# A graph network in four layers: the node pass between second and third layer taken out, edge states kept densely, the third layer in two stages

## The chip, the cores and the metric

The kernel runs on one core of a Trainium2 chip. The metric is the device time of one execution in microseconds (us), the median of several runs. The engines of the core are PE (matrix multiplication and transposes), DVE (vector), ACT (scalar, with tables for its functions), POOL (general) and SP (issues DMAs only). They run their own instruction streams and wait for one another by semaphores.

## The reference

There are 100,000 nodes with 64 numbers each and 50,000 edges, sorted by destination. Four layers follow one another, each of them as x = x + layer(relu(layernorm(x))):

```
x = x + gat(h, edges)                       # layer 0: softmax over the edges of a destination, tanh
x = x + gelu(batchnorm(gatv2(h)) + h)       # layer 1: softmax by destination, 16 edge attributes
x = x + rpe(h):                             # layer 2: softmax by SOURCE, 18 edge attributes
    qkv = h @ qkv_w + qkv_b
    compat = (q[s]*scale + ea @ q_rpe) . (k[t] + ea @ k_rpe)
    attn = segment_softmax(compat, s);  out = segment_sum((v[t] + ea @ v_rpe) * attn, s)
x = x + rgcn(h):                            # layer 3: twice a sum of messages by destination and a GRU,
    msg = (h[src] @ weight[type]) * norm;  state = gru(segment_sum(msg, dst), state)
    batchnorm over all nodes
```

The batch norms of layers 1 and 3 need a mean and a variance over all nodes, so what follows them can only start when every edge of the layer is done. A node without edges in a layer still gets the layer's value for an empty sum.

## The kernel before, in words

Edges are taken in chunks of CE = 512: 128 partitions with TPC = 4 edges each, 98 chunks (NCH). Nodes are taken in 32 chunks of 3200: 128 partitions with 25 rows each. Each stage below is one block of the program; the next one starts when it has ended. In a stage every engine has a loop over the chunks, written with `slots(eng, total, lags, body)`: in turn n the body is called with chunk n, n-1, n-2 and so on, so that the steps of neighbouring chunks overlap. The order of instructions on an engine is the order of the lines in its body; nothing reorders it.

The stages are: preparation (lists of edges by destination and by source, sorted on the chip); `conv_gat` (layer 0); `conv_gatv2` (layer 1); `nodes_second`, a pass over all nodes; `conv_rpe` (layer 2); `conv_first` and `conv_rgcn` (layer 3, in two rounds, called l3a and l3b in the traces); `nodes_last`, a pass over all nodes.

Rows of a node table are fetched by POOL with indirect DMAs (`Rows.gather`, L864), four to a chunk and list, and written back by indirect DMAs (`Scatter.scatter`, L897), four to a chunk. Both have four buffers. All other transfers are issued by SP, one after another in the order of its body; the last pass stores from ACT.

`conv_gatv2` gathers x1 by source, takes the destination's state from the last stage, computes attention, and scatters the result o1 to the nodes; it sums o1 and its squares for the batch norm. On its way it joins the 18 edge attributes with the destination numbers in one table (L1378, L1379) and fills two other tables with rest values. `nodes_second` loads x1 and o1 of every node, makes the layer norm of x1, the batch norm of o1, their sum, the Gelu and x2, and stores x2 twice (table x2, and the left half of table xh). Beside it POOL gathers the attributes of the edges in the order by source (L1559). `conv_rpe` gathers x2 of source and of the other end (two lists, in the order by source), norms them, multiplies with qkv_w (L1755) and the edge attributes with the position weights (L1756), makes the softmax by source with scans on DVE (L739, L813), adds x2, makes the layer norm of the result as well and scatters both as 128 numbers to xh. `conv_first` gathers 64 normed numbers from xh and does the first round of layer 3; `conv_rgcn` the second, and scatters its states to g2. `nodes_last` loads xh and g2 and stores the output.

In `Norm`, `square` (L675) runs on ACT, `rsqrt` (L685, L686) on ACT as Ln and Exp; `load_ln_exp` (L203) loads the table of these two functions.

## Time and profile before

| what | value |
|---|---|
| runs | 7380.1, 7376.67, 7300.94 us; median 7376.67 us |
| profiled execution | 7345.78 us, its span 7344.1 us |
| busy: PE, DVE, ACT, POOL | 3808.4 (52%), 5219.6 (71%), 2420.3 (33%), 5506.7 us (75%) |
| DMA | 647.68 MB, 88 GB/s mean, 846543 packets, 656112 of them under 512 B |
| chain that ended last | only the end of the last pass: DMA 2%, POOL 1%, DVE 1% |

The busy shares are means over stages which have different limits. Since a stage starts when the one before it has ended, the span is the sum of the stages, and each stage can be read by itself from its own stretch of time. The span minus the sum of the windows is below 0.2 us; the profiled execution's time is 1.7 us longer than its span.

### The profile page before, as it was taken

How to read it: one execution, taken by the hardware profiler on the slowest of the kernel's cores; microseconds unless marked ns; L12 is line 12 of the kernel's file. 1: busy time of each engine (PE TensorE's matmuls, PEld its weight loads, DVE VectorE, ACT ScalarE, POOL GpSimd, SP SyncE). 2: the span in 40 equal slices, each digit the busy share in tenths (PEclk: the TensorE clock that was granted, in tenths of full speed). 3: DMA queues.
4: the chain of work that ended last, by engine and by line, in shares of the span. 5: the costliest groups of instructions: out<-in, count | busy, mean ns of one | idle time of the engine just before them, and what ended most of it. 6: DMA issues, size and time to landing. Idle time of an engine off the chain costs nothing. (4 is left out here: it accounts for less than half of the span.)

```text
span 7344.1 us, 70844 instructions
## 1 busy us (share of the span) xinstructions
PE 3808.4 (52%) x11974; PEld 2014.6 (27%) x11974; DVE 5219.6 (71%) x9194; ACT 2420.3 (33%) x5053; POOL 5506.7 (75%) x5757
## 2 busy tenths in 40 slices
PE   0103444553677777000166666666668877777700
PEld 0001111111233333000044444444434434444400
DVE  5885777776799998898066666666667767777644
ACT  1113444443444444333033333333323323333300
POOL 4777888887677777788778888888667767777745
PEclk9999555555677777555555555555589988888855
DMA  3442222222454544676111111111123322222258
GB/s 98 133 126 66 73 73 73 73 74 69 117 122 122 122 122 126 185 217 174 14 44 41 43 41 43 43 41 43 38 69 90 89 63 48 48 48 48 47 175 247
DMA packets 846543, 647.68 MB, mean 88 GB/s; under 512 B 656112, under 2 KB 684269, under 8 KB 846271
## 3 DMA queue, kind: packets, MB, share of 16 engines
q1 hardware_dynamic: 691399, 463.53, 22.5%
q0 software_dynamic: 150560, 157.85, 10.3%
q10 hardware_dynamic: 4512, 25.60, 1.1%
q14 instruction: 59, 0.48, 0.0%
q8 instruction: 13, 0.21, 0.0%
HBM read 385.69 MB, written 274.56 MB: 90 GB/s over the span
## 5 line engine op out<-in xcount | busy, mean ns | idle before, releaser
L864 POOL DMA_INDIRECT l_rows<-x,l_num x1176 | 1241.0, 1055 | 333.3 <-issue 324.1
L1559 POOL DMA_INDIRECT er_edge_rows<-eat,all_perm x392 | 539.3, 1376 | 144.9 <-issue 131.4
L897 POOL DMA_INDIRECT xh<-l_out,l_snum x392 | 432.3, 1103 | 162.9 <-issue 104.8
L864 POOL DMA_INDIRECT l_rows<-in_x,l_num x392 | 440.5, 1124 | 106.3 <-issue 90.6
L1102 POOL DMA_INDIRECT pre_src_rows<-in_x,all_idx_src x392 | 396.8, 1012 | 163.9 <-issue 130.3
L897 POOL DMA_INDIRECT x<-l_out,l_snum x392 | 410.2, 1047 | 106.6 <-issue 89.4
L864 POOL DMA_INDIRECT l3a_rows<-xh,l3a_num x392 | 389.3, 993 | 133.7 <-issue 98.1
L897 POOL DMA_INDIRECT o<-l_out,l_snum x392 | 393.8, 1005 | 122.8 <-issue 104.7
L897 POOL DMA_INDIRECT g<-l3b_out,l3b_snum x392 | 393.5, 1004 | 107.0 <-issue 89.1
L864 POOL DMA_INDIRECT l3b_rows<-g_rows,l3b_num x392 | 386.7, 987 | 106.2 <-issue 91.7
L1729 PE MATMUL l_p_ea<-all_ident,l_ea 128*32 128x128 f32 x392 | 99.1, 406 | 704.6 <-ACT l_ea L1644 697.9
L1288 PE MATMUL l_p_hT<-all_ident,l_h 128*128 128x128 f32 x392 | 109.4, 435 | 528.2 <-DVE l_h L671 528.2
L675 ACT ACTIVATE l_n_sq<-l_n_cen 128x512 f32<-128x512 f32 (+1 forms) x392 | 223.9, 571 | 353.8 <-DVE l_n_cen L662 284.0
L1747 PE MATMUL l_p_score<-l_vT,all_w_head 68*128 68x512 f32 x196 | 200.3, 1126 | 265.2 <-DVEq L746 265.2
L821 PE MATMUL l_p_sums<-all_ident,l_sums 128*128 128x128 f32 x1176 | 300.0, 405 | 47.9 <-DVE l_sums L783 32.3
L1756 PE MATMUL l_p_qkv<-all_w_rpe,l_eaT 19*128 19x128 f32 x784 | 310.5, 497 | 0.0
L1755 PE MATMUL l_p_qkv<-all_w_qkv,l_hT 128*128 128x128 f32 x784 | 296.1, 481 | 0.9 <-ACT l_hT L1662 0.9
L2135 PE MATMUL l3b_p_gate<-all_w_gate,l3b_acc 128*128 128x256 f32 x784 | 284.5, 526 | 20.3 <-DVEq L2086 18.6
L2182 POOL TENSOR_TENSOR dl_xin<-dl_xin,all_shift 128x1600 f32<-128x1600 f32 x32 | 150.8, 4721 | 175.9 <-DMA dl_gin<-g 175.8
L2127 PE MATMUL l3b_p<-all_ident,l3b_hm 128*128 128x128 f32 x392 | 138.9, 370 | 257.3 <-DVEq L2079 257.3
L821 PEld LDWEIGHTS l_p_sums<-all_ident,l_sums 128*128 128x128 f32 x1176 | 203.5, 205 | 226.7 <-DVE l_sums L783 191.9
L1741 PE MATMUL l_p_hT<-all_ident,l_h 128*128 128x128 f32 x392 | 100.0, 405 | 312.2 <-DVEq L1708 312.2
(384 smaller groups left out, 12444.3 us busy)
## 6 DMA issues: line engine op xcount, KB each, us to landing
l_far<-far_d SPq DMA_DIRECT2D x196, 256.0 KB, 3.5
x<-ts_row SPq DMA_DIRECT2D x31, 812.5 KB, 4.4
d_xrow<-x SPq DMA_DIRECT2D x31, 812.5 KB, 4.5
l_far<-far_s SPq DMA_DIRECT2D x98, 256.0 KB, 3.4
o<-l_fill_o SPq DMA_DIRECT2D x97, 256.0 KB
g<-l_fill SPq DMA_DIRECT2D x97, 256.0 KB
xh<-l_fill_h SPq DMA_DIRECT2D x97, 256.0 KB
ts_xin<-in_x SPq DMA_DIRECT2D x31, 800.0 KB, 5.8
```

Source lines behind the costliest of these rows:

```text
L675: act.activation(self.sq[:], self.cen[:], ACT.Square).then_inc(self.squared, 1)
L821: ins = pe.transpose(self.p_sums[:, j * P:(j + 1) * P], self.sums[k.u][:, j * P:(j + 1) * P], c.ident[:])
L864: pool.indirect_dma_start(self.buf[k.q][:, j, at:at + w], None, table, bass.IndirectOffsetOnAxis(ap=self.num[k.q][:, m, j:j + 1], axis=0)) ...
L897: pool.indirect_dma_start(self.table, bass.IndirectOffsetOnAxis(ap=self.num[k.q][:, j:j + 1], axis=0), self.out[k.q][:, j, 0:self.cols], N ...
L1102: pool.indirect_dma_start(c.src_rows[:, t, :], None, x, bass.IndirectOffsetOnAxis(ap=c.idx_src[:, t:t + 1], axis=0)).then_inc(c.src_gather ...
L1559: pool.indirect_dma_start(c.edge_rows[:, t, :], None, eat, bass.IndirectOffsetOnAxis(ap=c.perm[:, t:t + 1], axis=0)).then_inc(c.edges_gath ...
L1747: pe.matmul(p_score[:], c.w_head[:], vT[k1.u][:], start=True, stop=True).then_inc(m["scored"], 1)
L1755: pe.matmul(p_qkv[:, at], hT[:, at], c.w_qkv[:], start=True, stop=False)
L1756: ins = pe.matmul(p_qkv[:, at], eaT[0:19, at], c.w_rpe[:], start=False, stop=True)
L2127: pe.transpose(p_01[:, cols], hm[:, j, 0:P], c.ident[:])
L2135: ins = pe.matmul(p_gates[:, j, :], acc[k1.u][:, j * P:(j + 1) * P], w_gate[:], start=True, stop=True)
L2182: pool.tensor_tensor(xin[k.u][:], xin[k.u][:], over_rows(c.shift3[0:NP, :], NR), ALU.add).then_inc(pool_done, 1)
```

## The change

The change takes `nodes_second` out and makes what it computed where it is needed:

- `conv_gatv2` no longer scatters o1. It stores three dense tables in the order of the edges by destination: xs (the gathered x1 of source and destination with its position), hs (their normed states) and eo1 (the result of the destination after each edge). It does not fill tables and does not join attributes. h has two buffers.
- A new stage `conv_edges` (l2 in traces) goes over the edges by destination. It gathers eo1 for the source of each edge, loads the other five inputs densely, makes batch norm, Gelu, x2 and its layer norm for both ends of each edge, carries the destination's row along with a scan, multiplies qkv and position weights, and stores x2 of both ends (x2e) and, for each edge, value and compatibility (vc_rows, 68 numbers).
- A new stage `conv_source` (l2s) gathers vc_rows in the order by source, makes the softmax and scatters the message sum to m2. Beside it, a class `Default` makes x2 for all nodes as if they had no edge in layer 1 (8 rows in each partition per turn) and stores it with the rest state of layer 3 to xg.
- `conv_first` gathers m2, adds the dense x2, and makes the layer norm. `conv_second` (the former second round) scatters x2 and state together, 128 numbers, to xg. `nodes_last` reads xg and m2 and has three operations in place of two on DVE.

The diff, cut to its core (`hold` is a wait together with an instruction that does nothing):

```diff
 def conv_gatv2 ... SP:
+                        if not k.round:
+                            hold(sp, rows.rows_free, k.n - 4)
+                            hold(sp, rows.saved[k.q], 16 * k.r)
...
+                    if old:
+                        hold(sp, rows.rows_free, old.n)
+                        sp.dma_start(edge_rows(xs, old), rows.buf[old.q][:]).then_inc(rows.saved[old.q], 16)
+                        hold(sp, m["h_ready"], old.n)
+                        sp.dma_start(edge_rows(hs, old), h[old.u][:]).then_inc(h_saved[old.u], 16)
+                    if older:
+                        hold(sp, kept.out_ready, older.n)
+                        sp.dma_start(edge_rows(eo1, older), kept.out[older.q][:, :, 0:D]).then_inc(o_saved[older.q], 16)
 POOL:
-                gather_scatter(pool, c, rows, sct, 7)
+                gather_scatter(pool, c, rows, None, 0)
 ACT:
-                act.wait_ge(attr_loaded, 32)
-                act.activation(attr_out[:, :, 0:ATTR], attr_in[:], ACT.Copy).then_inc(attr_joined, 1)
...
-def nodes_second(nc, c, x1, o1, x2, xh, eat):
...
-def conv_rpe(nc, c, dram, x2, xh):
...
+def conv_edges(nc, c, dram, eo1, xs, hs, edge_attr, x2e, vc_rows):
+        vc = [s.sb(f"vc{u}", [P, TPC, VC]) for u in range(2)]
...
 conv_edges, SP:
+                def body(k, _1, old, _3, _4, older):
+                    if k:
+                        ea.load(sp, c, k)
+                        if not k.round:
+                            hold(sp, rows.rows_free, k.n - 4)
+                        sp.dma_start(rows.buf[k.q][:, :, D:P], edge_rows(eo1, k)).then_inc(own_loaded[k.q], 16)
...
+                        sp.dma_start(x1[k.u][:], edge_rows(xs, k)).then_inc(x1_loaded[k.u], 16)
+                    if old:
+                        hold(sp, m["x2_ready"], old.n)
+                        sp.dma_start(edge_rows(x2e, old), x2[old.u][:]).then_inc(x2_saved[old.u], 16)
+                    if older:
+                        hold(sp, m["vc_ready"], older.n)
+                        sp.dma_start(edge_rows(vc_rows, older), vc[older.u][:]).then_inc(vc_saved[older.u], 16)
+                slots(sp, c.NCH, 5, body)
...
 conv_edges, ACT:
+                def body(k0, k1, k2):
+                    if k2:
+                        act.wait_ge(m["h_turned"], k2.n)
+                        act.activation(hT[k2.u][0:D, :], p_hT[0:D, :], ACT.Copy).then_inc(m["src_out"], 1)
+                    if k1:
+                        norm.square(act, k1.n)
+                        ea.copy_out(act, k1.n)
+                        norm.rsqrt(act, step, c, k1.n)
+                    if k2:
+                        act.wait_ge(m["qkv_done"], k2.n)
+                        if not k2.first:
+                            act.wait_ge(m["vc_ready"], k2.n - 2)
+                            act.wait_ge(vc_saved[k2.u], 16 * k2.t)
+                        v = p_qkv[:].rearrange("p (j f) -> p j f", j=TPC)
+                        act.activation(qk[k2.u][:], v[:, :, 0:D], ACT.Copy)
+                        act.activation(vc[k2.u][:, :, 0:D], v[:, :, D:P], ACT.Copy).then_inc(m["qkv_out"], 1)
+                    if k0:
+                        act.wait_ge(m["z_ready"], k0.n)
+                        act.activation(z[:], z[:], ACT.Gelu).then_inc(m["gelu_done"], 1)
+                        load_ln_exp(nc, act)
...
 conv_edges, PE:
+                def body(k1, k2):
+                    if k2:
...
+                            pe.matmul(p_qkv[:, at], hT[k2.u][:, at], c.w_qkv[:], start=True, stop=False)
+                            ins = pe.matmul(p_qkv[:, at], ea.T[0:ATTR + 1, at], c.w_rpe[:], start=False, stop=True)
+                        ins.then_inc(m["qkv_done"], 1)
+                    if k1:
+                        ea.turn(pe, c, k1)
+                        hold(pe, m["h_ready"], k1.n)
...
 class EdgeAttr, load(sp, c, k), the first transfer of SP's turn:
-            sp.wait_ge(self.turned, k.n - 2)
+            hold(sp, self.turned, k.n - 2)
...
+def conv_source(nc, c, dram, vc_rows, m2, x1, xg):
...
 conv_source, DVE:
+                def body(k0, k1, k2):
+                    if k1:
+                        bg.add(dve, step, k1)
+                    if k0:
+                        bg.center(dve, step, k0)
+                    if k1:
+                        dve.wait_ge(m["scored"], k1.n)
+                        sm.maxima(dve, step, k1, p_score[:])
+                    if k2:
+                        sct.free(dve, k2)
+                        sm.divide(dve, step, k2.n, sct.out[k2.q][:])
+                        dve.sem_inc(sct.out_ready, 1)
+                    if k0:
+                        bg.norm.add_up(dve, step, k0.n)
+                    if k1:
+                        sm.add_up(dve, step, k1, lambda p_: dve.tensor_tensor(p_, p_, vT[k1.u][0:D, :], ALU.mult))
+                    if k0:
+                        bg.arg(dve, step, c, k0)
...
 conv_first, DVE:
+                        step(dve.tensor_tensor(x3[:], rows.buf[k0.q][:], x2[k0.u][:], ALU.add))
+                        norm.center(dve, step, x3[:])
...
+                        norm.add_up(dve, step, k0.n)
```

Two places show how the order of instructions differs. The names in brackets are those of the first user of a semaphore number, so they tell that a row waits, and not for what; the diff tells that.

SP, before: the end of `nodes_second` and the start of `conv_rpe`, whose SP does nothing but load one row of flags (far_s) for each chunk.

```order
L1551 DMA xh<-d_out 3200x1x64
L1550 DMA x<-d_out 32x1600 [waits q_turned]
L1551 DMA xh<-d_out 800x1x64
L1539 UNCONDITIONAL_BRANCH [waits setup_step,setup_trans]
L1622 UNCONDITIONAL_BRANCH [waits barrier_Pool_Activation_PE_DVE_SP_release]
L719 DMA l_far<-far_s 128x512 x2
L719 DMA l_far<-far_s 128x512 [waits ts_stored0] x2
```

SP, now: one turn of `conv_edges` in its steady part (l_rows<-eo is the destination's own eo1, l_keep the flags of the scan).

```order
L955 DMA l_ea<-in_edge_attr 128x4x18 [waits q_turned]
L1575 DMA l_rows<-eo 128x4x64 [waits setup_prods]
L1578 DMA l_h_1<-hs 128x4x128 [waits l0_pos_put]
L1581 DMA l_keep<-keep_d 64x512 [waits l0_exp2]
L1585 DMA l_x_1<-xs 128x4x130 [waits l0_odd_step]
L1588 DMA x2e<-l_x_1 128x4x128 [waits l0_odd_step]
L1591 DMA vc_rows<-l_vc 128x4x68 [waits l0_valued]
```

In place of one transfer in a turn there are seven, each behind a wait of its own: first the edge attributes, last the store of vc.

ACT, before: one turn of `conv_rpe`, from the copy of vT to the two copies of qkv out of PSUM.

```order
L1653 ACTIVATE l_vT<-l_p_vT 68x512 [waits l0_fill_o_done,l0_e_stored2]
L1656 ACTIVATE l_eaT<-l_p_ea 32x512 [waits l0_arg_ready]
L685 ACTIVATE l_n_lnv<-l_n_var,all_eps 128x8 [waits prep_loaded]
L686 ACTIVATE l_n_rstd<-l_n_lnv 128x8 [waits l0_tanh_ready]
L675 ACTIVATE l_n_sq<-l_n_cen 128x256 [waits ts_no_pos]
L1662 ACTIVATE l_hT<-l_p_hT 128x512 [waits l0_scored]
L808 ACTIVATE l_ex<-l_ex 128x1024 [waits ts_stored0]
L685 ACTIVATE l_n_lnv<-l_n_var,all_eps 128x4 [waits ts_zeroed]
L686 ACTIVATE l_n_rstd<-l_n_lnv 128x4 [waits l0_tanh_ready]
L1670 ACTIVATE l_x_keep<-l_x_near 128x256 [waits l0_near_exped]
L1676 ACTIVATE l_qk<-l_p_qkv 128x256 [waits l0_e_stored2,l0_h_turned]
L1677 ACTIVATE l_vc<-l_p_qkv 128x4x64
```

ACT, now: one turn of `conv_edges`, from the copy of hT to the second table load.

```order
L1616 ACTIVATE l_hT<-l_p_hT 64x512 [waits l0_tanh_ready]
L672 ACTIVATE l_n_sq<-l_n_cen 128x512 [waits setup_trans]
L972 ACTIVATE l_eaT<-l_p_ea 32x512 [waits q_turned]
L682 ACTIVATE l_n_lnv<-l_n_var,all_eps 128x8 [waits setup_loaded]
L683 ACTIVATE l_n_rstd<-l_n_lnv 128x8 [waits ts_xin_loaded0]
L1627 ACTIVATE l_qk<-l_p_qkv 128x256 [waits ts_piece_done,l0_valued,l0_arg_ready]
L1628 ACTIVATE l_vc<-l_p_qkv 128x4x64
L1630 REGISTER_ALU
L1631 ACT_TABLE_LOAD
L1631 ACTIVATE l_z<-l_z 128x512 [waits l0_pos_put]
L203 ACT_TABLE_LOAD
```

The softmax's Exp and the second norm have gone to other stages; a Gelu between two table loads has come in behind the qkv copies, and the copy to qk has three waits in place of two.

## Rows read from the trace of the kernel before

**Rows 1.** windows of whole stages, core 0; PEclk 1.00 is 2.4 GHz
```profile
core 0: us, PE busy (x) PEld busy (x) DVE busy (x) ACT busy (x) POOL busy (x), PEclk, DMA share, GB/s
0.00:1823.70 1823.70, 644.19 (x1377) 255.34 (x1377) 1339.71 (x2764) 598.71 (x1320) 1388.34 (x1411) 0.71 0.29 85
1823.70:2953.90 1130.20, 804.34 (x2553) 362.54 (x2553) 979.70 (x1682) 526.35 (x1085) 850.70 (x982) 0.70 0.49 121
2953.90:3631.00 677.10, 0.00 (x0) 0.00 (x0) 467.02 (x256) 197.85 (x192) 539.26 (x392) 0.50 0.58 158
3631.00:5372.00 1741.00, 1123.75 (x3332) 703.65 (x3332) 1146.47 (x2058) 581.72 (x1471) 1345.92 (x1471) 0.52 0.17 41
5372.00:5971.80 599.80, 494.20 (x1960) 263.76 (x1961) 427.09 (x890) 194.82 (x393) 408.95 (x491) 0.98 0.34 86
5971.80:7010.00 1038.20, 741.88 (x2752) 429.33 (x2752) 709.79 (x1480) 320.81 (x592) 822.71 (x980) 0.82 0.24 47
7010.00:7344.00 334.00, 0.00 (x0) 0.00 (x0) 149.83 (x64) 0.00 (x0) 150.81 (x32) 0.50 0.79 230
```

**Rows 2.** lines by form, conv_gatv2: busy, mean ns | idle before
```profile
L897 POOL DMA_INDIRECT o<-l_out,l_snum x392 | 393.8, 1005 | 122.8 <-issue 104.7 <-DVE l_out L803 16.4 <-POOL l_snum L887 1.2
L1467 DVE TENSOR_TENSOR_SCAN l_hT<-l_keep,l_end_T,l_p_hT 64x512 f32<-64x512 f32 x98 | 126.0, 1286 | 11.1 <-PE l_p_hT L1497 8.6
...
L675 ACT ACTIVATE l_n_sq<-l_n_cen 128x512 f32<-128x512 f32 x98 | 60.0, 612 | 0.0
L969 ACT ACTIVATE l_eaT<-l_p_ea 32x512 f32<-32x512 f32 x98 | 57.5, 587 | 2.4
L685 ACT ACTIVATE l_n_lnv<-l_n_var,all_eps 128x8 f32<-128x8 f32 x98 | 29.5, 301 | 64.2 <-DVE l_n_var L667 64.2
L1378 ACT ACTIVATE l_attr_out<-l_attr_in 100x9000 f32<-100x9000 f32 x1 | 7.7, 7704 | 23.3 <-DMA l_dst_in<-in_dst 23.3
```

**Rows 3.** timeline of conv_rpe: start, length, engine, line [idle before <-releaser]
```profile
4605.40 1.01 PE L1729 MATMUL l_p_ea<-all_ident,l_ea 128*32 128x128 f32 x4
...
4616.03 0.63 PE L1755 MATMUL l_p_qkv<-all_w_qkv,l_hT 128*128 128x128 f32 x2
...
4621.77 0.38 ACT L1676 ACTIVATE l_qk<-l_p_qkv 128x256 f32<-128x256 f32 x1 [5.89 <-PE l_p_qkv L1756]
```

**Rows 4.** timeline of SP in conv_gatv2, one turn
```profile
2411.62 0.34 SPq L719 DMA_DIRECT2D l_far<-far_d  x1
...
2415.44 0.51 SPq L1344 DMA_DIRECT2D l_rows<-e  x1
```

**Rows 5.** DMA issues: count, KB each, median us to landing
```profile
e<-l_out SPq DMA_DIRECT2D x98, 128.0 KB, 2.0
l_rows<-e SPq DMA_DIRECT2D x98, 128.0 KB, 3.1
```

**Rows 6.** lines, nodes_second
```profile
L1594 ACT ACTIVATE d_y<-d_y 128x1600 f32<-128x1600 f32 x32 | 49.2, 1537 | 181.6 <-DVEq L1582 181.6
L203 ACT ACT_TABLE_LOAD x32 | 41.1, 1283 | 0.6
L1594 ACT ACT_TABLE_LOAD x32 | 41.1, 1283 | 0.6
```

**Rows 7.** timeline of ACT in conv_first, its start
```profile
5395.65 1.28 ACT L1902 ACT_TABLE_LOAD   x1
5396.95 0.60 ACT L1902 ACTIVATE l3a_gru_e<-l3a_p_gate 128x512 f32<-128x512 f32 x1
```

**Rows 8.** lines by form, conv_rpe
```profile
L864 POOL DMA_INDIRECT l_rows<-x,l_num x784 | 824.9, 1052 | 224.9 <-issue 219.4 <-ACTq L1650 4.6 <-POOL l_num L852 0.9
L897 POOL DMA_INDIRECT xh<-l_out,l_snum x392 | 432.3, 1103 | 162.9 <-issue 104.8 <-DVEq L1718 56.8 <-POOL l_snum L887 1.0
...
L745 DVE TENSOR_TENSOR l_ex<-l_ex,l_top 128x512 f32<-128x512 f32 x98 | 67.8, 692 | 3.4
L831 DVE TENSOR_TENSOR l_out<-l_p_sums,l_rden 128x256 f32<-128x256 f32 x98 | 41.6, 425 | 3.4
```

More of the change, by code:

```diff
@@ L443, in _ @@
                         layout = need
-                for _ in range(3):
+                for _ in range(2):
                     n += 1
@@ L1511, in body @@
                         hold(pe, m["sums_ready"], k3.n)
-                        stat.add(pe, last, sct.out[k3.q], m["sums_added"])
+                        stat.add(pe, last, kept.out[k3.q], m["sums_added"])
                     if k0:
@@ new lines, with __init__, parts, nodes @@
+class Default:
+    R = 8
+    def __init__(self, s, c, table, out):
+        self.table, self.to = table, out
+        self.x = [s.sb(f"bg_x{u}", [P, self.R, POS + D]) for u in range(2)]
+        self.y = s.sb("bg_y", [P, self.R, D])
+        self.row = [s.sb(f"bg_row{u}", [P, self.R, P]) for u in range(2)]
+        self.norm = Norm(s, "bg", self.R)
+        self.loaded = [s.sem(f"bg_loaded{u}") for u in range(2)]
+        self.saved = [s.sem(f"bg_saved{u}") for u in range(2)]
+        self.made, self.arg_ready, self.gelu_done, self.done = (s.sem("bg_" + n) for n in ("made", "arg_ready", "gelu_done", "done"))
+        self.rest = (c.N - (c.NCH - 1) * P * self.R) // self.R
+        assert 0 < self.rest <= P and c.N % self.R == 0
+    def parts(self, k):
+        return self.rest if k.last else P
+    def nodes(self, table, k):
+        n = self.parts(k)
+        return table[bass.ds(k.i * (P * self.R), n * self.R), :].rearrange("(p r) f -> p r f", r=self.R)
+    def make(self, pool, c):
+        for u in range(2):
+            pool.tensor_copy(self.row[u][:, :, D:P], over_rows(c.quiet[1][:], self.R)).then_inc(self.made, 1)
+    def load(self, sp, k):
+        if not k.first:
+            hold(sp, self.done, k.n - 2)
+        sp.dma_start(self.x[k.u][0:self.parts(k)], self.nodes(self.table, k)).then_inc(self.loaded[k.u], 16)
+    def store(self, sp, k):
+        if k.start:
+            sp.wait_ge(self.made, 2)
+        hold(sp, self.done, k.n)
+        sp.dma_start(self.nodes(self.to, k), self.row[k.u][0:self.parts(k)]).then_inc(self.saved[k.u], 16)
+    def finish(self, sp, c):
+        for u in range(2):
+            sp.wait_ge(self.saved[u], 16 * c.NCH // 2)
+    def center(self, dve, step, k):
+        dve.wait_ge(self.loaded[k.u], 16 * (k.t + 1))
+        self.norm.center(dve, step, self.x[k.u][:, :, POS:POS + D])
+    def arg(self, dve, step, c, k):
+        self.norm.scale(dve, step, k.n, self.y[:])
+        step(dve.tensor_tensor(self.y[:], self.y[:], over_rows(c.shift1[:], self.R), ALU.add))
+        dve.sem_inc(self.arg_ready, 1)
+    def add(self, dve, step, k):
+        if not k.first:
+            dve.wait_ge(self.saved[k.u], 16 * k.t)
+        dve.wait_ge(self.gelu_done, k.n)
+        step(dve.tensor_tensor(self.row[k.u][:, :, 0:D], self.y[:], self.x[k.u][:, :, POS:POS + D], ALU.add))
+        dve.sem_inc(self.done, 1)
+    def gelu(self, act, k):
+        act.wait_ge(self.arg_ready, k.n)
+        act.activation(self.y[:], self.y[:], ACT.Gelu).then_inc(self.gelu_done, 1)
@@ L1621, in conv_rpe @@
+def conv_source(nc, c, dram, vc_rows, m2, x1, xg):
+    with Scope(nc, "l2s") as s:
+        rows = Rows(s, [(vc_rows, VC, 0, c.perm)], VC)
+        sct = Scatter(s, m2, D, c.scat_s, c.N)
+        sm = Softmax(s)
+        bg = Default(s, c, x1, xg)
+        vT = [s.sb(f"vT{u}", [VC, CE]) for u in range(2)]
+        p_vT, p_score = s.ps("p_vT", (VC, CE)), s.ps("p_score")
+        m = s.sems("dve_step act_step vT_ready scored")
         with nc.Block() as block:
@@ L1840, in _, with conv_first @@
                     gru.update(dve, step, k + 1, one(c.quiet[0]) if k else None, one(c.quiet[k]))
-def conv_first(nc, c, name, dram, table, g_rows):
+def conv_first(nc, c, name, dram, m2, x2e, g_rows):
     with Scope(nc, name) as s:
-        rows = Rows(s, [(table, P, 0, c.idx_src)], P)
+        rows = Rows(s, [(m2, D, 0, c.idx_src)], D)
+        x2 = [s.sb(f"x2_{u}", [P, TPC, D]) for u in range(2)]
+        x3 = s.sb("x3", [P, TPC, D])
+        norm = Norm(s, "n", TPC)
         kept = Kept(s, D)
@@ L2245, in gnn @@
             prep_lists(nc, c, a["src"], a["dst"], a["edge_weight"], a["edge_type_3"], dram, beside)
-          conv_gat(nc, c, a["x"], dram, x1, e1, o1)
-        conv_gatv2(nc, c, dram, x1, e1, o1, a["edge_attr_16"], g2, a["edge_attr_18"], a["dst"], eat, xh)
-        with Scope(nc, "er") as er:
-            c.edge_rows = er.sb("edge_rows", [P, c.NT, EAW])
-            c.edges_gathered = er.swdge_sem("edges_gathered")
-            nodes_second(nc, c, x1, o1, x2, xh, eat)
-            conv_rpe(nc, c, dram, x2, xh)
-        conv_first(nc, c, "l3a", dram, xh, g_rows)
-        conv_rgcn(nc, c, "l3b", dram, g_rows, 1, g_rows, g2)
-        nodes_last(nc, c, xh, g2, out)
+          conv_gat(nc, c, a["x"], dram, x1, e1, m2)
+        conv_gatv2(nc, c, dram, x1, e1, eo1, a["edge_attr_16"], xs, hs)
+        conv_edges(nc, c, dram, eo1, xs, hs, a["edge_attr_18"], x2e, vc_rows)
+        conv_source(nc, c, dram, vc_rows, m2, x1, xg)
+        conv_first(nc, c, "l3a", dram, m2, x2e, g_rows)
+        conv_second(nc, c, "l3b", dram, g_rows, x2e, xg)
+        nodes_last(nc, c, xg, m2, out)
 def kernel(**inputs):
```

678 lines of the change are left out of this document (315 added, 363 removed).

## Prediction

> **What bounds the kernel now.** I read the windows of whole stages first [rows 1]; they add up to the span of 7344.1 us, and the profiled execution took 7345.78 us, 0.4% below the median of the runs, so sums against it stand for that median within their spread of 1.1%. No engine bounds the program: each stage is a pipeline over 98 chunks (node stages: 32) with a period of its own, and a change is worth what it does to the period of the stage it touches, times 98. Dividing windows by 98: conv_gatv2 11.5 us, of which DVE is busy 10.0; conv_rpe 17.8, POOL 13.7 busy and ready to issue most of the rest; conv_first 6.1; conv_rgcn 10.6, POOL 8.4 busy. The node stages (677.1 and 334.0 us) have DMA shares of 0.58 and 0.79. TensorE's granted clock is 0.52 in conv_rpe, the lower of the two levels, where PE works in bursts and waits between them; 0.98 in conv_first.
>
> **What goes and what is cheap.** nodes_second goes: −677 us [rows 1]. That is the largest gain and the surest; but its work returns, below.
>
> The preparation loses two DVE operations and a flip: 0, because POOL's gathers of source rows end that stage. conv_gat fills another table of the same size: 0. So 1823.7 us stay.
>
> conv_gatv2 loses its scatter on POOL, 393.8 + 122.8 us [rows 2], but DVE sets its period (10.0 busy of 11.5), and DVE keeps the same operations; bounds 0 and −120 (down to DVE's 980 plus a head of 30). At the head ACT waits 23.3 us for the 18-wide edge attributes and copies them for 7.7 [rows 2]; that goes. The dense stores ride on SP: seven transfers in a turn at the spacing of [rows 4] (3.82 us for five steps, 0.76 each) take 5.3 us of an 11 us period. I take −40: **1090**.
>
> **The new stage conv_edges** has 98 chunks. Work of each engine, per chunk: DVE a scan 1.29 [rows 2], eight operations of 0.69 [rows 8], three small ones of about 0.3: 7.7. ACT six copies and squares (0.6 for 512 wide, 0.38 for 256 [rows 2, 3]), Ln and Exp 0.3 each, a Gelu taken as 0.61 like other operations of 512 columns, and two table loads of 1.283 [rows 6], because Gelu and Ln/Exp alternate: 6.4. POOL one list of four gathers, 4 × (1052 + 287 ns) = 5.4 [rows 8]. No engine fills 10 us. The period is set by a wait that before.py has nowhere: vc has two buffers, and ACT, before it copies chunk j+2 out of PSUM (L1627), waits until SP has stored chunk j. SP issues that store last in the turn of chunk j+5, and that turn begins by waiting for PE's transpose of the edge attributes of j+3, which PE runs right after the qkv matmuls of j+2. These are the very matmuls whose result ACT wants to copy. So each period holds, one after another:
> - hT copy 0.59 [rows 2]; qkv at the lower clock, from the first matmul to ACT's copy, 4616.03 to 4621.77: 5.74; the four attribute transposes 1.01 [rows 3];
> - SP's turn: six spacings of 0.76 before the seventh transfer, 4.58 [rows 4]; its landing: between 2.0 (a 128 KB store) and 3.1 (a transfer that also comes last in a turn of six) [rows 5], taken as 2.5, since the six ahead of it carry 1.1 MB;
> - ACT's two copies 0.76 [rows 3], table load 1.28, Gelu 0.61, table load 1.28, and only then the next hT copy;
> - three hand-overs between engines, which no row isolates, taken as 0.3 each (an estimate).
>
> Sum 19.2 us, or 98 × 19.2 + 27 for head and drain = **1909**. Behind the waiting ACT stand Gelu, on which DVE's next x2 waits, and the next hT copy, on which PE waits; behind SP's wait stand all five loads, but they are for a chunk that is needed later. PE then works 7.8 us of 19.2 in one burst, so I take the lower clock, as in conv_rpe.
>
> On the table loads a row comes first: in nodes_second 64 of them took 1283 ns each with 0.6 us of idle ahead of 32 [rows 6], and in conv_first the load begins at 5395.65 and the next operation at 5396.95, 1.30 later [rows 7]. So I charge the load and nothing more. The Trainium skill, "ScalarE: Activation LUTs", section "What ACT_TABLE_LOAD costs", adds a drain of about 1380 ns to every switch, 2.66 us in all; both loads lie on the chain above, so by that rule the sum would be 2 × 1.38 × 98 = 270 us longer (an estimate from that page). [rows 7] shows no such gap.
>
> **The new stage conv_source** keeps conv_rpe's softmax, one gather and the scatter: POOL 4 × (1052 + 287) + 4 × (1103 + 415) ns = 11.4 us [rows 8]. DVE has two scans 2.56, four operations of the softmax at 0.69, a quotient 0.43, three small ones about 0.6, and the node defaults that nodes_second used to make, now six operations of 0.69 in every chunk: 10.5, with 16 gaps of 0.035 (3.4 us in 98 [rows 8]) 11.0. So 407 us of nodes_second's 467 us of DVE work come back here, on the path. Bounds 10.9 and 12.5; I take 11.8 (both engines near 11.4, each waiting for the other a little), 98 × 11.8 + 24 = **1180**.
>
> **conv_first** had no normalization; now x3 = gathered + dense part and its layer norm are made here. DVE 427.09/98 = 4.36, plus four operations of 256 columns at 0.425 [rows 8], plus gaps 0.45: 6.5; ACT 1.99 + two table loads, a square, Ln, Exp: 5.6 [rows 1, 2, 6]. The period of before is 1.7 longer than DVE's work in it; with a third of that kept it is 7.1, 98 × 7.1 + 24 = **720**, against 599.8. If PE's clock falls with the longer pauses, PE's 5.0 us at 0.98 grow to as much as 10: up to 950; if the norm hides fully, 650.
>
> **conv_second** scatters 128-wide rows instead of 64: 1103 against 1005 ns [rows 2, 8], 392 times, at most +38 us on POOL, which bounds it; half is taken: **1050**. **nodes_last** moves 3.2 MB for each full node chunk in place of 2.4: DMA-bound, between 0 and a third more; as xg comes in long runs in place of 256-byte pieces I take +16: **350**.
>
> **Sum.** 1823.7 + 1090 + 1909 + 1180 + 720 + 1050 + 350 + 1.7 (around the span) = 8124. Against 677 us saved and 40 in conv_gatv2 stand 1348 us more in the third attention stage (3089 for 1741), 120 in conv_first, 28 in the last two. Forecast **8120 us**, 10.5% slower than the profiled execution, 10.1% than the median.
>
> **The rivals.**
> 1. *The loop holds, but PE gets the upper clock* in conv_edges (as conv_first has): the 6.75 us of PE halve, 15.8 us a period, 1575: total 7790. For it: the qkv burst is dense. Against: conv_rpe has the same burst at 0.52.
> 2. *The store lands in time*, because SP runs ahead and does not wait for the transpose. Then a shorter loop is left: scan 1.29, qkv 5.74, transposes 1.01, eaT copy 0.59, Ln and Exp 0.6, two operations on DVE 0.9, transposes of h 1.0, eight hand-overs 0.25: 13.1 us at the lower clock, 1311: total 7526, 2% slower.
> 3. *On the other side: faster.* With the same early store, PE's pauses get short and the clock rises, so that 7.8 us of PE halve: 9.2, and with DVE's 7.7 plus waits about 9.8, 987 us: total 7202, 2% faster. It decides below 11.4 us a period, where conv_edges and conv_source together cost what is saved elsewhere. It needs the store 4 to 6 us earlier than the row spacing of SP allows; the place to look is ACT's idle time ahead of L1627.
> 4. *Each table load drains ACT first*, as a mechanism of this kernel: both loads on the loop of conv_edges are longer by what ACT needs to run empty. Rows give idle of 0.02 ahead of a load [rows 6] to 1.30 from load to next operation [rows 7], so next to nothing; if the load were paid twice in each switch, 2 × 1.28 × 98 = 251: total 8375. This is the rule of the Trainium skill's page above, whose own figure gives 8394.
> 5. *The change does not do what it says*: the node pass is not gone but moved, as priced in conv_source. Should POOL's waits hide it fully, conv_source falls to 10.9, −88 us, which stays inside the forecast's own range of 7930 to 8300.
>
> **How the numbers follow.** Forecast (with 5) 0.68, first rival 0.12, second 0.08, third 0.08, fourth 0.04. The predicted time is the forecast's. The range leaves out rivals 2, 3 and 4, 0.20 together, and takes in rival 1 and the bounds of landing, conv_first and conv_source: 7720 to 8330. About 1% is what a measurement of this kernel can tell from no change. Faster by more: most of rival 3, 0.06; within: the rest of it and a part of rival 2, 0.04; slower: 0.90.
>
> **What would show it.** In the profile after: no nodes_second; a conv_edges window near 1900 us with PE's clock near 0.5; ACT's L1627 idle for some 7 to 8 us a chunk, with a DMA (vc_rows) as releaser or, by the last event, one of SP's turn; SP issuing seven transfers in a burst right behind PE's attribute transposes, once a period. The forecast is wrong if L1627 waits for PE alone, if the burst of SP begins ahead of the qkv matmuls, if conv_source is far from 1180, or if conv_first's clock falls.

## The result and the profile after

The changed kernel took 8316.79 us (median; 8310.51 to 8321.02), the kernel before 7360.27 us beside it. The ratio is 1.1314, 95% interval 1.1244 to 1.1384: 13% slower. The forecast was 8120 us, in a range of 7720 to 8330.

The windows of whole stages after, of the profiled execution (columns as in [rows 1]). The third row is conv_edges, the fourth conv_source, the fifth conv_first:

```profile
0.00:1817.40 1817.40, 645.33 (x1371) 254.46 (x1371) 1336.34 (x2759) 597.86 (x1319) 1381.73 (x1407) 0.69 0.30 85
1817.40:2914.20 1096.80, 811.81 (x2555) 365.65 (x2555) 979.14 (x1687) 519.24 (x1085) 420.53 (x493) 0.70 0.52 121
2914.20:4872.20 1958.00, 772.65 (x2353) 503.65 (x2353) 742.62 (x1186) 597.00 (x986) 428.18 (x493) 0.50 0.31 68
4872.20:6137.70 1265.50, 393.68 (x980) 187.29 (x980) 1016.22 (x1568) 576.62 (x785) 1019.37 (x982) 0.50 0.34 100
6137.70:6940.10 802.40, 561.33 (x1960) 304.54 (x1960) 583.38 (x1282) 668.78 (x984) 404.45 (x490) 0.90 0.28 64
6940.10:7994.50 1054.40, 760.44 (x2752) 432.05 (x2752) 703.21 (x1480) 322.22 (x593) 822.72 (x980) 0.80 0.34 68
7994.50:8319.00 324.50, 0.00 (x0) 0.00 (x0) 225.14 (x96) 0.00 (x0) 122.43 (x32) 0.50 0.82 316
```

Against [rows 1]: the first two layers are as before but for 33 us less in conv_gatv2 (1130.2 to 1096.8); nodes_second (677.1) is gone; conv_rpe's 1741.0 have become 1958.0 + 1265.5; conv_first has grown from 599.8 to 802.4; conv_second and nodes_last moved by +16 and −10. conv_edges is the longest stage, and in it no engine is busy for half the time: PE 39%, DVE 38%, ACT 30%, POOL 22%, at the lower of PE's two clocks.

Who waits for whom in conv_edges shows in its groups by line (busy, mean ns of one | idle before, and what ended it):

```profile
L203 ACT ACT_TABLE_LOAD x99 | 127.0, 1283 | 1.8
L1631 ACT ACT_TABLE_LOAD x98 | 125.7, 1283 | 1.8
...
L972 ACT ACTIVATE l_eaT<-l_p_ea 32x512 f32<-32x512 f32 x98 | 57.5, 587 | 593.5 <-PE l_p_ea L967 593.5
L1627 ACT ACTIVATE l_qk<-l_p_qkv 128x256 f32<-128x256 f32 x98 | 37.6, 383 | 685.3 <-DMA vc_rows<-l_vc 678.3 <-PE l_p_qkv L1708 7.0
```

ACT's copy of qk out of PSUM (L1627) is idle for 685.3 us ahead, 7.0 a chunk, and 678.3 of them end with the transfer vc_rows<-l_vc: the store of the chunk two before. In conv_rpe the same copy waited for PE alone [rows 3]. One period, first ACT (start, length, [idle before <-releaser]):

```profile
3907.58 0.59 ACT L1616 ACTIVATE l_hT<-l_p_hT 64x512 f32<-64x512 f32 x1
...
3915.46 0.59 ACT L972 ACTIVATE l_eaT<-l_p_ea 32x512 f32<-32x512 f32 x1 [6.18 <-PE l_p_ea L967]
...
3923.46 0.38 ACT L1627 ACTIVATE l_qk<-l_p_qkv 128x256 f32<-128x256 f32 x1 [6.99 <-DMA vc_rows<-l_vc]
...
3924.14 1.28 ACT L1631 ACT_TABLE_LOAD   x1
3925.43 0.63 ACT L1631 ACTIVATE l_z<-l_z 128x512 f32<-128x512 f32 x1
3926.08 1.28 ACT L203 ACT_TABLE_LOAD   x1
3927.37 0.59 ACT L1616 ACTIVATE l_hT<-l_p_hT 64x512 f32<-64x512 f32 x1
```

then PE, its first qkv matmul and the transposes of the edge attributes behind the last:

```profile
3908.63 0.77 PE L1707 MATMUL l_p_qkv<-all_w_qkv,l_hT 128*128 128x128 f32 x2 [10.05 <-ACT l_hT L1616]
...
3914.39 1.03 PE L967 MATMUL l_p_ea<-all_ident,l_ea 128*32 128x128 f32 x4
```

and SP, the first and the last of the seven transfers of its turn:

```profile
3915.65 0.40 SPq L955 DMA_DIRECT2D l_ea<-in_edge_attr  x1
...
3919.82 0.40 SPq L1591 DMA_DIRECT2D vc_rows<-l_vc  x1
```

Read in order of time this is a ring without a break. hT is copied at 3907.58, PE begins qkv at 3908.63 and the attribute transposes at 3914.39; they end at 3915.42. Only then, at 3915.65, does SP issue the first transfer of its turn, and at 3919.82 the seventh, the store of vc. ACT, which had its qkv result at 3914.4, goes on at 3923.46 when that store has landed, then makes two copies, a table load, the Gelu and a table load, and copies the next hT at 3927.37. The period is 19.79 us: 1.05 + 5.76 + 1.03 + 0.23 + 4.17 + 3.64 + 0.68 + 3.23.

### The profile page after: what moved, and what is told of

Read it like the earlier page. It is cut to its first block and busy times, and to the rows that moved or that the text cites. A ratio compares the mean times of both kernels' runs of the same rounds, so it can differ in the third digit from the quotient of the medians.

```text
span 8319.0 us, 78500 instructions
## 1 busy us (share of the span) xinstructions
PE 3945.2 (47%) x11971; PEld 2047.6 (25%) x11971; DVE 5586.0 (67%) x10058; ACT 3281.7 (39%) x5752; POOL 4599.4 (55%) x4877
## 5 line engine op out<-in xcount | busy, mean ns | idle before, releaser
L864 POOL DMA_INDIRECT l2s_rows<-vc_rows,l2s_num x392 | 544.0, 1388 | 106.2 <-issue 104.4
L1871 PE MATMUL l2s_p_score<-l2s_vT,all_w_head 68*128 68x512 f32 x196 | 200.4, 1126 | 649.6 <-DVEq L743 648.8
L864 POOL DMA_INDIRECT l_rows<-in_x,l_num x392 | 443.0, 1130 | 106.2 <-issue 90.7
L900 POOL DMA_INDIRECT m<-l2s_out,l2s_snum x392 | 423.9, 1081 | 128.8 <-issue 91.5
L864 POOL DMA_INDIRECT l_rows<-x,l_num x392 | 398.5, 1017 | 153.6 <-issue 94.6
L864 POOL DMA_INDIRECT l3a_rows<-m,l3a_num x392 | 385.5, 983 | 150.8 <-issue 95.2
L900 POOL DMA_INDIRECT xg<-l3b_out,l3b_snum x392 | 394.1, 1005 | 114.3 <-issue 88.5
L864 POOL DMA_INDIRECT l_rows<-eo,l_num x392 | 376.7, 961 | 132.9 <-issue 94.6
L1707 PEld LDWEIGHTS l_p_qkv<-all_w_qkv,l_hT 128*128 128x128 f32 x784 | 196.3, 311 | 1030.8 <-issue 1030.8
L972 ACT ACTIVATE l_eaT<-l_p_ea 32x512 f32<-32x512 f32 x196 | 115.0, 587 | 597.5 <-PE l_p_ea L967 595.2
L672 ACT ACTIVATE l_n_sq<-l_n_cen 128x512 f32<-128x512 f32 x294 | 183.5, 624 | 348.7 <-DVE l_n_cen L659 292.0
L1627 ACT ACTIVATE l_qk<-l_p_qkv 128x256 f32<-128x256 f32 x98 | 37.6, 383 | 685.3 <-DMA vc_rows<-l_vc 678.3
```

Source lines behind the costliest of these rows:

```text
L672: act.activation(self.sq[:], self.cen[:], ACT.Square).then_inc(self.squared, 1)
L864: pool.indirect_dma_start(self.buf[k.q][:, j, at:at + w], None, table, bass.IndirectOffsetOnAxis(ap=self.num[k.q][:, m, j:j + 1], axis=0)) ...
L900: pool.indirect_dma_start(self.table, bass.IndirectOffsetOnAxis(ap=self.num[k.q][:, j:j + 1], axis=0), self.out[k.q][:, j, 0:self.cols], N ...
L972: act.activation(self.T[:], self.p[:], ACT.Copy).then_inc(self.ready, 1)
L1707: pe.matmul(p_qkv[:, at], hT[k2.u][:, at], c.w_qkv[:], start=True, stop=False)
L1871: pe.matmul(p_score[:], c.w_head[:], vT[k0.u][:], start=True, stop=True).then_inc(m["scored"], 1)
```

## The experiments

All were made to tell apart what sets the period of conv_edges first, then of conv_source and conv_first. Each window row below has the columns of [rows 1]. A stage that an edit leaves alone came out the same from run to run within 1 us (conv_source, 1265.5 to 1266.3), 5 us (conv_first, 798.0 to 802.7) or 7 us (conv_edges, 1952.3 to 1958.5), so the windows of single runs can be compared.

**Four buffers for vc.**

```diff
-        vc = [s.sb(f"vc{u}", [P, TPC, VC]) for u in range(2)]
+        vc = [s.sb(f"vc{q}", [P, TPC, VC]) for q in range(4)]
...
-                            act.wait_ge(vc_saved[k2.u], 16 * k2.t)
+                        if not k2.round:
+                            act.wait_ge(vc_saved[k2.q], 16 * k2.r)
...
```

> vc gets four buffers in place of two; nothing else changes. Theory (a closed loop: qkv, attribute transposes, SP's turn, landing of the vc store, ACT's copies, Gelu between two table loads): the copy out of PSUM no longer waits for a store of this period, its idle time ahead (685 us in 98 chunks) falls below 100 us, and the shorter loop over the attribute transposes, Ln, Exp and the transposes of h sets the period: about 13.1 us, conv_edges 1958 -> about 1310, total 8317 -> about 7670. Rival 1 (SP's seven transfers with their waits are the bound whatever the buffers): conv_edges falls by less than 100 us. Rival 2 (PE's clock rises as soon as its pauses shrink): period about 9.8 us, conv_edges about 990, total about 7350.

conv_edges, window, and then three rows of ACT's timeline in one period (its L1629 is the copy of qk, L972 that of the edge attributes):

```profile
2917.50:4188.50 1271.00, 772.62 (x2353) 503.59 (x2353) 742.70 (x1185) 588.51 (x985) 428.79 (x491) 0.50 0.50 105
```

```profile
3507.53 0.59 ACT L972 ACTIVATE l_eaT<-l_p_ea 32x512 f32<-32x512 f32 x1 [4.76 <-PE l_p_ea L967]
...
3508.51 0.38 ACT L1629 ACTIVATE l_qk<-l_p_qkv 128x256 f32<-128x256 f32 x1
...
3509.19 1.28 ACT L1633 ACT_TABLE_LOAD   x1
```

Measured 7632.53 us, 1.0389 of the kernel before (1.0355 to 1.0424); conv_edges 1271.0 us, 687 less (about 1310 was expected). The copy of qk follows Exp with no idle time. The ring was the cause, and rivals 1 and 2 of this run fall: SP issued as many transfers as before, and PE's clock stayed at 0.50. The period left is 12.7 us, and the rows point to ACT's own order, which was tested further below. ACT stands waiting at the eaT copy until 3507.53, when PE has done qkv and the transposes, and only then come Ln, Exp, copies, table load, Gelu, table load and the next hT copy.

**Two buffers, the store first in SP's turn.** The two lines of the store (`hold(sp, m["vc_ready"], older.n)` and its transfer) move ahead of `ea.load(sp, c, k)`.

> vc keeps two buffers; its store moves from the last to the first place of SP's turn, ahead of the load of the edge attributes, so it no longer stands behind the wait for the transposes. Theory (position in SP's turn is what holds the store up): as with four buffers, period about 13.1 us, conv_edges about 1310. Rival (two buffers are too few in any order, since a store takes 3.9 us to land): conv_edges stays above 1700.

```profile
2918.80:4191.20 1272.40, 772.63 (x2353) 503.62 (x2353) 742.71 (x1185) 589.55 (x986) 428.28 (x491) 0.50 0.50 105
```

7639.53 us; conv_edges 1272.4, the same as with four buffers. In this order SP issues the store of a chunk one turn earlier, before it waits for PE again. Two buffers are enough; it was the place behind the wait for PE's transposes that held the store.

**No Gelu in conv_edges.**

```diff
-                        act.activation(z[:], z[:], ACT.Gelu).then_inc(m["gelu_done"], 1)
-                        load_ln_exp(nc, act)
+                        act.activation(z[:], z[:], ACT.Copy).then_inc(m["gelu_done"], 1)
```

> Left out: the Gelu of conv_edges is a Copy, so the two table loads of each chunk go there; the rest stays. Theory (both loads lie on the closed loop and cost what their rows show, 1.283 us): 2 x 1.283 x 98 = 252 us less, conv_edges 1958 -> about 1705. Rival (a switch costs 2.66 us with a drain, by the Trainium skill, ScalarE: Activation LUTs, What ACT_TABLE_LOAD costs): about 520 us less, 1440. Rival 2 (the loads are hidden beside the store's landing): under 30 us.

```profile
2913.90:4627.90 1714.00, 772.58 (x2353) 503.58 (x2353) 742.62 (x1185) 322.00 (x790) 427.27 (x491) 0.50 0.37 78
```

conv_edges 1714.0 us, 244 less: 196 loads at 1.245 us each (the Copy took 631 ns where the Gelu took 629). Both loads stood on the ring, at about the price of their rows. The Trainium skill's drain of 1380 ns ("ScalarE: Activation LUTs", "What ACT_TABLE_LOAD costs") would have given some 520 (an estimate from that page); the measurement decides against it here.

**Sigmoid ahead of tanh in conv_first.** The profile after had a surprise there, three table loads in each chunk where two were counted:

```profile
L203 ACT ACT_TABLE_LOAD x102 | 130.9, 1283 | 23.3 <-PEq L64 21.4
L2029 ACT ACT_TABLE_LOAD x98 | 125.7, 1283 | 1.7
L2024 ACT ACT_TABLE_LOAD x98 | 125.7, 1283 | 1.7
```

The edit swaps the two `if` parts of ACT's body (`if k3:` with the tanh, `if k2:` with the sigmoid).

> In conv_first ACT's sigmoid stands ahead of the tanh of the chunk before, in place of behind it; the two don't depend on each other. The trace after has three table loads in each chunk there (ahead of tanh, of sigmoid, of Ln/Exp), where conv_rgcn and the stage of before need none between sigmoid and tanh. Theory (ACT is the bound of conv_first: idle 1.0 of 7.8 us, and the set loaded for sigmoid holds tanh as well): one load less, conv_first 802 -> about 690, limited then by DVE's 6.0 us and gaps. Rival (PE at a granted clock of 0.90 or the chain between engines is the bound): less than 30 us change.

```profile
6133.60:6939.30 805.70, 585.54 (x1960) 323.95 (x1960) 583.58 (x1282) 541.37 (x887) 405.37 (x490) 0.86 0.28 64
```

The load ahead of the tanh went (ACT busy 668.8 to 541.4 us), and conv_first did not move: 805.7 us. The theory that ACT bounds it is wrong, as ACT then idles more. What bounds it instead was tested further below.

**ACT's order in conv_edges** (on four buffers). In ACT's body Ln and Exp, then the Gelu between its loads, go ahead of `ea.copy_out`:

```diff
                         norm.square(act, k1.n)
-                        ea.copy_out(act, k1.n)
                         norm.rsqrt(act, step, c, k1.n)
...
+                    if k0:
+                        act.wait_ge(m["z_ready"], k0.n)
+                        act.activation(z[:], z[:], ACT.Gelu).then_inc(m["gelu_done"], 1)
+                        load_ln_exp(nc, act)
+                    if k1:
+                        ea.copy_out(act, k1.n)
```

> Built on the kernel with four vc buffers. In conv_edges ACT's order changes: Ln and Exp of the norm, then the Gelu between its two table loads, come ahead of the copy of the transposed edge attributes, so both fall in the 4.8 us that ACT waits for PE there; nothing is added or left out. Theory (with the store out of the way ACT's own order closes the next loop: qkv 5.76, transposes 1.03, eaT copy, Ln, Exp, copies, table load, Gelu, table load, hT copy = 12.7 us): the period falls to about 10, set by qkv 5.76 + transposes 1.03 + 1.09 + scan 1.28 + hand-overs, with DVE's 7.6 us and its gaps close behind; conv_edges 1271 -> about 1000, or less if PE's clock rises. Rival (the rest of the period is DMA: the seven transfers and a gather take 0.50 of the 16 engines already at 12.7): not below 1150.

```profile
2916.80:3971.00 1054.20, 772.25 (x2353) 503.99 (x2353) 743.83 (x1185) 583.85 (x986) 436.87 (x491) 0.50 0.59 127
```

conv_edges 1054.2 us, 10.5 a period, and 7407.48 us in all: 54 more than expected, but far below the rival's 1150. The order on ACT was the second ring.

**The node operation later in conv_source.** `bg.add(dve, step, k1)` moves behind `sm.maxima`. In the profile after, the stage had these rows:

```profile
L864 POOL DMA_INDIRECT l2s_rows<-vc_rows,l2s_num x392 | 544.0, 1388 | 106.2 <-issue 104.4 <-POOL l2s_num L850 1.5 <-PE l2s_p_vT L1866 0.3
L900 POOL DMA_INDIRECT m<-l2s_out,l2s_snum x392 | 423.9, 1081 | 128.8 <-issue 91.5 <-DVEq L1849 23.3 <-POOL l2s_snum L888 14.1
...
L1776 DVE TENSOR_TENSOR l2s_bg_row<-l2s_bg_y,l2s_bg_x 128x512 f32<-128x512 f32 x98 | 67.8, 692 | 82.5 <-ACT l2s_bg_y L1781 82.5
```

> On the changed kernel: in conv_source DVE's last operation on the node defaults (behind ACT's Gelu, waited for 0.84 us in each chunk) moves behind the softmax's maxima. Theory A (DVE's chain is the bound of conv_source, 12.7 us = 10.4 busy + 0.84 wait + 1.4 gaps): conv_source 1265 -> about 1185. Theory B (POOL is the bound: its gathers of 272-byte rows take 1388 ns here against 961 in conv_edges, and it waits for nobody in the steady part): no change, under 15 us.

```profile
4873.30:6100.90 1227.60, 393.72 (x980) 187.37 (x980) 1017.35 (x1568) 576.95 (x785) 959.23 (x982) 0.50 0.35 103
```

38 us less (1265.5 to 1227.6; 8278.63 in all): half of what theory A gave, and more than theory B. DVE's wait for ACT is gone, and POOL waits for DVE for 45.4 us where it was 23.3. The run by itself does not choose one bound; the next one and POOL's timeline do.

**No node computation in conv_source.** What stays of it are the stores of constants.

> Left out: the computation of the node defaults in conv_source (DVE's six operations, ACT's five and its two table loads in each chunk, the loads of x1); constants are stored in their place. It tells what the node pass costs where it was put. Theory A (DVE's chain is the bound): DVE falls to about 7 us a chunk with gaps, POOL's instructions return to about 1.0 us because DVE presses less, and POOL's 8 x 1.3 us set about 10.7: conv_source 1265 -> about 1070, so the node pass costs about 200 of the 677 us saved. Theory B (POOL's longer gathers belong to the rows of 272 bytes): conv_source stays above 1230.

```profile
4869.90:6003.90 1134.00, 396.97 (x980) 183.96 (x980) 612.55 (x980) 161.57 (x197) 909.77 (x984) 0.50 0.30 89
```

```profile
L900 POOL DMA_INDIRECT m<-l2s_out,l2s_snum x392 | 437.1, 1115 | 107.0 <-issue 79.5 <-POOL l2s_snum L888 17.1 <-PE l2s_p_vT L1852 10.4
L864 POOL DMA_INDIRECT l2s_rows<-vc_rows,l2s_num x392 | 389.5, 994 | 106.2 <-issue 89.3 <-POOL l2s_num L850 16.0 <-DMA l2s_rows<-vc_rows,l2s_num 0.6
```

conv_source 1134.0 us, 131.5 less, and POOL's gathers take 994 ns in place of 1388. POOL is busy or between two of its own instructions for 1112 of 1134 us (909.8 + 107.0 + 106.2, less 11.0 in which it waits for others), so it is the bound without the node pass. In the changed kernel the same sum is 1230.8 of 1265.5 us (1019.4 + 128.8 + 106.2, less 23.6), so it is the bound there too. Theory B has this bound right and its reason wrong, as the same rows of 272 bytes now take 994 ns. Theory A has it right that DVE's work lengthens POOL's; its 1070 was too low by 64 us, since the scatters took 1115 ns and POOL's copies of its index lists, 82 us in the stage, stood in no sum.

This run took out ACT's operations and the loads of x1 as well. That it is DVE which makes POOL's transfers long shows in the changed kernel's timeline, in one chunk of conv_source (l2s_p_score lies in PSUM, the memory of PE's results; the other inputs of these rows lie in SBUF, the engines' own memory):

```profile
5512.34 1.28 DVE L810 TENSOR_TENSOR_SCAN l2s_sums<-l2s_ex,l2s_sums 128x512 f32<-128x512 f32 x1
5512.51 1.94 POOL L864 DMA_INDIRECT l2s_rows<-vc_rows,l2s_num  x1 [0.16 <-issue]
...
5516.02 0.69 DVE L1776 TENSOR_TENSOR l2s_bg_row<-l2s_bg_y,l2s_bg_x 128x512 f32<-128x512 f32 x1 [0.83 <-ACT l2s_bg_y L1781]
5516.34 1.19 POOL L864 DMA_INDIRECT l2s_rows<-vc_rows,l2s_num  x1 [0.30 <-issue]
...
5518.61 1.28 DVE L736 TENSOR_TENSOR_SCAN l2s_top<-l2s_far,l2s_top,l2s_p_score 128x512 f32<-128x512 f32 x1
5519.46 1.00 POOL L900 DMA_INDIRECT m<-l2s_out,l2s_snum  x1 [0.17 <-POOL l2s_snum L888]
...
5523.32 0.69 DVE L676 TENSOR_REDUCE l2s_bg_var<-l2s_bg_sq 128x8 f32<-128x512 f32 x1 [0.22 <-DVE l2s_out L828]
5523.67 0.97 POOL L900 DMA_INDIRECT m<-l2s_out,l2s_snum  x1 [0.30 <-issue]
```

The eight transfers of this chunk fall in two groups. Five begin while DVE is in an operation with two inputs in SBUF; they end 0.82 to 0.87 us after that operation and take 1.19 to 1.94 us. The other three begin during a scan with one input in PSUM, a reciprocal and a reduction, and take 0.97 to 1.00 us. The longest is held by the softmax's own scan (L810), so a move of one operation on DVE, as in the run before, changes which transfers are held and for how long. This is read from timelines; no edit tested it by itself.

**A combination.** Four buffers, ACT's order, the late node operation, and in conv_edges DVE's `norm.scale` with `h_ready` ahead of the product of qk.

> Four vc buffers, ACT's new order in conv_edges, the late node operation in conv_source (all measured one by one), and one more: in conv_edges DVE scales h ahead of the compatibility product instead of behind it, since PE's transposes of h waited 0.96 us for DVE in each chunk there (row of the kernel with ACT's new order). Nothing is left out. Theory: 7406 - 38 (conv_source) - 0.8 x 98 (conv_edges 1054 -> about 975) = about 7290, 0.8% faster than the kernel before. Rival (DVE, with 7.6 us and 2 us of gaps, is already the bound of conv_edges): conv_edges stays above 1035, total about 7365, no difference from the kernel before.

```profile
2908.60:3916.20 1007.60, 753.09 (x2353) 513.21 (x2353) 742.75 (x1185) 584.30 (x987) 426.57 (x492) 0.50 0.63 132
```

7313.41 us against 7318.59, ratio 0.9991 (0.997 to 1.0012): no difference from the kernel before. conv_edges came to 1007.6 us, between the theory's 975 and the rival's 1035.

**No addition in conv_first** (on the kernel with the sigmoid first).

> Built on the kernel with the sigmoid first. Left out: in conv_first the addition of the dense x2 to the gathered rows (one DVE operation of 0.43 us with 0.25 to 0.32 of gap); the transfer of x2 stays. Theory (DVE is the bound of conv_first: 6.0 us of operations and 1.8 us of gaps between them, most of 0.15 to 0.32 where semaphore instructions stand between two operations): conv_first 806 -> about 735. Rival (the chain over PE and ACT sets the period and DVE's gaps are waits): less than 25 us.

```profile
6132.80:6887.60 754.80, 563.92 (x1960) 307.00 (x1960) 543.06 (x1184) 539.73 (x887) 407.41 (x490) 0.89 0.28 68
```

conv_first 754.8 us, 51 less than 805.7, about seven tenths of what was expected. So DVE is the bound up to there; in the changed kernel other engines and DMAs end only some 20 us of its idle time in the steady part of this stage. How its time goes shows in four steps of its timeline there:

```profile
6500.91 0.42 DVE L676 TENSOR_REDUCE l3a_n_var<-l3a_n_sq 128x4 f32<-128x256 f32 x1 [0.22 <-DVE l3a_out L2073]
6501.48 0.42 DVE L2079 TENSOR_TENSOR l3a_gru_arg<-l3a_gru_e,l3a_p_gate 128x256 f32<-128x256 f32 x1 [0.15 <-DVE l3a_n_var L676]
6501.94 0.42 DVE L2080 TENSOR_TENSOR l3a_gru_arg<-l3a_gru_arg,l3a_p_gate 128x256 f32<-128x256 f32 x1
6502.72 0.17 DVE L2047 TENSOR_TENSOR l3a_w<-all_wrel,l3a_n_rstd 128x12 f32<-128x12 f32 x1 [0.36 <-DVE l3a_gru_arg L2080]
```

Between operations stand 0.04 us where the body has nothing between them (6501.48 to 6501.94: 0.46 for an operation of 0.42) and 0.15 to 0.36 where the body has semaphore increments and waits between them. Of a period of 7.8 us DVE works 6.0.

**The combination with two edits more.** The table load of conv_edges goes from behind the Gelu to ahead of Ln, and POOL makes the addition in conv_first, one chunk ahead:

```diff
+                        load_ln_exp(nc, act)
                         norm.rsqrt(act, step, c, k1.n)
...
-                        load_ln_exp(nc, act)
...
+                        pool.tensor_tensor(x3[k1.u][:], rows.buf[k1.q][:], x2[k1.u][:], ALU.add).then_inc(m["x3_ready"], 1)
...
-                        step(dve.tensor_tensor(x3[:], rows.buf[k0.q][:], x2[k0.u][:], ALU.add))
```

> On the kernel that combines four vc buffers, ACT's order, DVE's order and the late node operation (7313 us). Nothing is left out. Two more edits: in conv_edges the load of the Ln/Exp table moves from behind the Gelu to just ahead of Ln, where ACT waits 1.9 us for DVE; in conv_first POOL adds the dense x2 to the gathered rows in place of DVE, one chunk ahead, and the sigmoid stands first. Theory (ACT's load ahead of hT still stands on conv_edges's loop, then qkv 5.76 + transposes 1.03 and 1.06 + scan 1.28 + hand-overs remain, 9.5 us; conv_first is bound by DVE): conv_edges 1008 -> about 960, conv_first 798 -> about 750 (the kernel without the addition had 755), total about 7215, 1.3% faster than the kernel before. Rival 1 (DVE's gaps hold conv_edges at 9.8 us or more): conv_edges above 990. Rival 2 (POOL's addition and DVE's operations slow each other, as POOL's gathers do in conv_source): conv_first stays above 785.

```profile
2919.70:3911.20 991.50, 768.01 (x2353) 503.75 (x2353) 743.20 (x1185) 573.07 (x987) 427.99 (x492) 0.50 0.63 135
...
5138.10:5909.40 771.30, 595.41 (x1960) 314.99 (x1960) 543.84 (x1184) 540.89 (x887) 471.31 (x588) 0.83 0.29 67
```

7264.96 us, 0.9895 of the kernel before (0.9856 to 0.9934): the same plan of stages, with its rings opened, is 1% faster than the kernel before, 50 us short of what was expected, and takes some 12.5% less than as it was changed. conv_edges 991.5 lies just above rival 1's border of 990, and conv_first 771.3 between the theory and rival 2. POOL's addition waits there for the load of x2, which has two buffers; DVE in turn waited for that addition for 10.4 us only, but for PE's messages for 54.0 us, where it was 6.5 in the changed kernel, at a granted clock of 0.83 in place of 0.90:

```profile
L2018 POOL TENSOR_TENSOR l3a_x<-l3a_rows,l3a_x 128x256 f32<-128x256 f32 x98 | 71.8, 732 | 149.3 <-DMA l3a_x<-x2e 149.2
...
L2070 DVE TENSOR_TENSOR_SCAN l3a_acc<-l3a_keep,l3a_acc,l3a_p_msg 64x512 f32<-64x512 f32 x97 | 123.4, 1272 | 69.7 <-PE l3a_p_msg L2112 54.0 <-DVE l3a_pair L2064 15.7
```

More buffers for x2 were not tried, and which of these waits holds the stage is not shown.

## Why the prediction held, and where its sizes failed

**The mechanism.** The step on which the forecast rested, the ring over SP's turn and the store of vc, is in the trace link by link, and two experiments that open it in different places both take out 686 us. PE's clock was 0.50 there, as taken. Of the signs that were named against the forecast, two appeared in part: conv_source is 7% above 1180, and conv_first's clock fell, from 0.98 to 0.90. DVE, the bound of conv_first, waited for PE's messages for only 6.5 us in that stage, so the clock is not what made it long.

**The sizes in conv_edges.** 1958 us measured for 1909. SP's six spacings took 4.17 us for 4.58; the copies 0.68 for 0.76; from the issue of the store to ACT's copy it took 3.64 us where 2.5 and a hand-over stood. The other links agree within 0.2 us. So the term that was too small is the landing: it was taken between two rows of transfers in a less loaded turn [rows 5]. In the profile after, it grows along the turn, from 2.3 us for the second transfer to 3.9 for the last, which is about as large (KB each, median us to landing):

```profile
vc_rows<-l_vc SPq DMA_DIRECT2D x98, 136.0 KB, 3.9
...
l_rows<-eo SPq DMA_DIRECT2D x98, 128.0 KB, 2.3
```

**conv_source**, 1265.5 for 1180: the term that failed is POOL's, priced with gathers of 1052 ns [rows 8]; they took 1388 here, 132 us more in 392 gathers, because of the operations of DVE that they meet. POOL's two copies of index lists in each chunk, 0.5 us, were left out of the sum too; against that, gaps and scatters came out 49 us shorter. And the sentence that 407 us of node work come back on the path is wrong: taken out, it gave back 131.5, since POOL's own work nearly fills that stage without it. So the node work costs 131.5 us in its new place, against the 677 us of nodes_second; what conv_edges does of it for the edges is not in this figure.

**conv_first**, 802.4 for 720: two steps failed. A third table load was not seen, but cost nothing (fourth experiment). And the sum had 1.0 us a chunk beside DVE's operations, 0.45 of gaps at 0.035 each and a third of the 1.7 us of the period before; it is 1.8 (7.8 less 6.0). At 98 chunks these 0.8 us are 78 of the 82 that were missing. That the semaphore instructions in the body make them is argued from the rows above alone.

**The rest.** conv_gatv2 1096.8 for 1090, conv_second 1054.4 for 1050 (half of its 38 us would have been 1057), nodes_last 324.5 for 350. conv_edges, conv_source and conv_first were short by 217 us together, the others too long by 20; that is the distance of the forecast. The time lies 13 us below the upper end of the range, so the range held by little: the direction and the ring were foretold, the sum of the stages with some luck.

**The rivals.** The first (upper clock) did not happen. The second (the store in time) is what the first two experiments made true: 7632 and 7640 us, for 7526 worked out. conv_edges itself came out shorter than the 1311 listed (1271, as ACT's order closed a ring of 12.7 us by other steps than the 13.1); the rest of the difference is what conv_source and conv_first were short. The third, faster than before, needed a conv_edges of 987 us; the last kernel reached 991.5 and is faster, but with PE's clock still at 0.50: by order, not by clock. The fourth fell with the third experiment. The fifth holds in part: of the node pass, 131.5 us came back in conv_source. What stays open is how short conv_source would be with POOL's transfers kept clear of DVE's operations with two inputs; no run did that.

## What to carry to other kernels

Before a stage is split, follow each buffer ring of the new stage through every engine and queue that it passes, in the order in which each issues its work: a store that is last in a turn which begins with a wait for the consumer's own work closes a ring, and the period is then the sum of all its links, however idle every engine is. If all engines of a stage are under half busy, look for the wait that ends last, and first change an order (a store to the head of its turn, a table load into an idle place) before adding buffers; here both gave some 686 us. And a pass that is removed is worth its window only if the stage that takes over its work had room for it.
